# A fused attention and expert layer on one core: VectorE's dependent instructions laced with others, and two sums handed to TensorE and ScalarE

## The reference

```
h = layernorm(x) * (1 + ca) + sa
x = x + ga * attention(h)
h = layernorm(x) * (1 + cb) + sb
x = x + gb * experts(h)
```

```
pos  = clip(base + s_idx * freq_avg + phase_avg, 0, L - 1)
g    = g_lo + frac * (g_hi - g_lo)
out  = silu(einsum('blshd,blhs->blhd', g, w) @ out_w.T)
```

```
logits = h @ router_w.T + router_b
mask   = one_hot(top_k(softmax(logits), 2)).sum
out    = einsum('bse,ehd,bsd->bsh', mask, expert_w, h) + mask @ expert_b
```

## Time and profile before

| | us |
|---|---|
| three runs | 307.86, 310.82, 311.46 (median 310.82) |
| the profiled execution | 308.9 |
| its span on the core | 307.0 |
| busy TensorE / VectorE / ScalarE / GpSimd | 257.3 / 277.2 / 229.4 / 38.8 |
| mean granted TensorE clock | 0.898 of full |

### The profile page before, as it was taken

The page is one execution under the profiler, slowest core; times in us unless marked ns, Lnnn a source line. Parts: engine busy times, 40 slices in busy tenths (PEclk is TensorE's granted clock), DMA queues, the critical chain, the costliest instruction groups (busy, mean ns, idle before and its releaser), DMA issues.

```text
span 307.0 us, 5136 instructions
## 1 busy us (share of the span) xinstructions
PE 257.3 (84%) x1720; PEld 189.1 (62%) x1720; DVE 277.2 (90%) x570; ACT 229.4 (75%) x636; POOL 38.8 (13%) x64
## 2 busy tenths in 40 slices
PE   6970971999489998999699989999899959888995
PEld 3530830874388477857597568747784758475664
DVE  7799988999979899999999999999999999991772
ACT  3585788799868998898869988998679656845301
POOL 6204001200410011002020011002200400001100
PEclk9596697599958999899969997999699989999999
DMA  5630000020002200140005000500003000400001
GB/s 170 206 97 0 2 0 0 0 71 1 1 2 61 96 1 0 36 138 3 0 1 174 0 0 2 168 8 1 0 37 137 2 1 20 155 0 2 26 9 53
DMA packets 12160, 12.91 MB, mean 42 GB/s; under 512 B 1171, under 2 KB 11110, under 8 KB 11366
## 3 DMA queue, kind: packets, MB, share of 16 engines
q1 hardware_dynamic: 11684, 12.18, 12.8%
q10 hardware_dynamic: 450, 0.40, 0.5%
HBM read 10.43 MB, written 2.15 MB: 41 GB/s over the span
## 4 chain that ended last, share of the span: by engine, by line
DVE 50%; PE 22%; issue 14%; ACT 11%; POOL 2%; DVEq 0%; ACTq 0%; POOLq 0%
DVE AT L788 18%; DVE T L751 12%; PE pT L974 4%; DVE hm L849 4%; PE pR L974 3%; PE pY L1054 3%; ACT c L471 2%; DVE x L805 2%; PE pE L1054 2%; ACT xn L391 2%; DVE endw L776 2%; PE pR L951 2%; DVE x L854 1%; ACT hT L414 1%; DVE prodF L764 1%
## 5 line engine op out<-in xcount | busy, mean ns | idle before, releaser
L751 DVE COPY_PREDICATED T<-mask,T 128x672 f32<-128x672 int16 (+11 forms) x54 | 83.3, 1543 | 0.8
L788 DVE TENSOR_TENSOR AT<-T,c 128x2064 f32<-128x2064 f32 x32 | 72.3, 2301 | 0.0
L488 ACT ACTIVATE A<-pT 128x512 f32<-128x512 f32 x64 | 36.1, 599 | 27.6 <-PE pT L974 27.1
L974 PE MATMUL pT<-first,AT 128*128 128x128 f32 x256 | 43.9, 328 | 13.1 <-DVE AT L796 13.0
L1054 PE MATMUL pE<-hm,late 128*128 128x256 f32 x224 | 52.6, 386 | 0.0
L974 PEld LDWEIGHTS pT<-first,AT 128*128 128x128 f32 x256 | 37.3, 173 | 17.2 <-DVE AT L796 15.5
L1054 PEld LDWEIGHTS pE<-hm,late 128*128 128x128 f32 x224 | 41.2, 190 | 6.6
L974 PE MATMUL pR<-first,AT 128*128 128x128 f32 x256 | 40.4, 311 | 0.0
L315 POOL TENSOR_SCALAR ve<-sq 128x4 f32<-128x4 f32 (+1 forms) x18 | 8.8, 487 | 245.8 <-ACT xn L361 202.2
L488 ACT ACTIVATE A<-pR 128x512 f32<-128x512 f32 x64 | 35.8, 611 | 3.7 <-PE pR L974 3.6
L974 PEld LDWEIGHTS pR<-first,AT 128*128 128x128 f32 x256 | 36.0, 165 | 0.0
(11 more groups left out here) (139 smaller groups left out, 370.9 us busy)
## 6 DMA issues: line engine op xcount, KB each, us to landing
mkb<-mask_rows SPq DMA_DIRECT2D x6, 1024.0 KB, 5.4
x<-in_x SPq DMA_DIRECT2D x7, 256.0 KB, 5.6
out<-x SPq DMA_DIRECT2D x7, 256.0 KB, 5.7
late<-in_late SPq DMA_DIRECT2D x1, 584.0 KB, 3.9
mkb<-mask_rows SPq DMA_DIRECT2D x1, 512.0 KB, 3.8
x<-in_x SPq DMA_DIRECT2D x2, 128.0 KB, 3.5
wmod<-in_wmod ACTq DMA_DIRECT2D x1, 256.0 KB, 3.6
out<-x SPq DMA_DIRECT2D x2, 128.0 KB, 3.3
```

Of the source, the lines that this page charges most:

```text
L488: nc.scalar.activation(A[b][:, m, 2 * j:2 * j + 2, :].rearrange("p h l -> p (h l)"), four_banks(k)[:, :], ACT.Copy).then_inc(a_A, 1)
L751: nc.vector.copy_predicated(rows[:, :, :, j0:j1], spread(mask[:, k, 0:w, j0:j1], [P, w, H, j1 - j0], 2), rows[:, :, :, j0 + (1 << bit):j1 ...
L788: nc.vector.tensor_tensor(AT[:, bt, :, :].rearrange("p h (j r) -> p h j r", r=BLK), spread(T[n % 2][:, bt, 0:H, 0:NB], [P, H, NB, BLK], 3) ...
L974: ins = nc.tensor.transpose(four_banks(k)[:, c0:c0 + P], AT[:, 2 * b + i, 2 * j + a, m * P:(m + 1) * P], ident)
```

## The change

Four things.

- *Order on VectorE.* `ends_of`, `products`, `grid`, `route`, `sum_ends` and `spread_out` are cut into smaller stages, and these are called in another order, so that between an instruction and the one that reads its result there stands another. The products follow the first AT copy, the two products of hm come before the fourth and fifth network stage, the residual after the fifth.
- *Hits.* hit has 24 columns per index (erow repeated three times), and mk is gone. TensorE's back_mk takes the two hits of a tile through two matmuls with the identity that add up in the bank.
- *Last sum.* For units 0 to 5, back_out adds x (through the identity) to the transposed moeT in the bank, with two matmuls per tile instead of one transpose; ScalarE copies the bank to x (`total` on ScalarE). Units 6 to 8 keep VectorE's sum.
- *Order and filling.* On ScalarE, stats2 comes after front_hs and sums1. On TensorE, four matmuls of zeros (bf16, 512 columns) stand between back_x2T and back_logits.

```diff
-    c["erow"] = np.broadcast_to(np.arange(E, dtype=np.float32), (P, E)).copy()
+    c["erow"] = np.broadcast_to(np.tile(np.arange(E, dtype=np.float32), NP), (P, NP * E)).copy()
...
             def store(n):
-                sp.wait_ge(v_out, n + 1)
+                if n < LATE - 1:
+                    sp.wait_ge(a_out, n + 1)
+                else:
+                    sp.wait_ge(v_out, n - LATE + 2)
...
+            def total(n):
+                act.wait_ge(t_out, n + 1)
+                nc.scalar.activation(of_x(n), moe_bank(n)[:, 0:tiles(n) * C].rearrange("p (a c) -> p a c", c=C),
+                                     ACT.Copy).then_inc(a_out, 1)
...
-                run(i, -1, stats2)
                 if i >= 0:
                     run(i, 1, front_hs)
                 run(i, 2, sums1)
+                run(i, -1, stats2)
...
                 run(i, -1, back_mk)
+                run(i, -2, total)
                 run(i, 2, norm1)
...
-                dve.wait_ge(v_hit, n + 1)
+            def hits(n):
+                w = tiles(n)
+                dve.wait_ge(v_topi, LT * before(n + 1))
                 if n > 0:
                     dve.wait_ge(t_mk, n)
-                nc.vector.tensor_tensor(mk[:, 0:w, :].rearrange("p a (k e) -> p a k e", e=E),
-                                        spread(hit[:, 0:w, 0, :], [P, w, NP, E], 2),
-                                        spread(hit[:, 0:w, 1, :], [P, w, NP, E], 2), ALU.add).then_inc(v_mk, 1)
+                nc.vector.tensor_tensor(hit[:, 0:w, :, :], spread(spread(erow, [P, 2, NP * E], 1), [P, w, 2, NP * E], 1),
+                                        spread(topi[:, 0:w, 0:2], [P, w, 2, NP * E], 3), ALU.is_equal).then_inc(v_hit, 1)
...
-                run(i, 0, network, range(0, 2))
+                run(i, 0, network, range(0, 1))
...
-                run(i, 0, sum_ends)
-                run(i, 0, network, range(2, 4))
+                run(i, 0, sum_ends, 0)
+                run(i, 0, network, range(1, 2))
+                run(i, 0, sum_ends, 1)
+                run(i, 0, network, range(2, 3))
                 run(i, -2, masked, 0)
+                run(i, 0, network, range(3, 4))
+                second(i, -2, masked, 1)
                 run(i, 0, network, range(4, 5))
                 run(i, -1, residual)
-                second(i, -2, masked, 1)
                 run(i, 0, network, range(5, 6))
                 run(i, 1, line)
+                run(i, 0, spread_out, 0)
+                run(i, 1, past_ends)
+                run(i, 0, spread_out, 1)
                 run(i, 1, ends_of)
-                run(i, 1, products)
-                run(i, 0, spread_out, 0)
+                run(i, 0, set_ends, 0)
+                run(i, 1, product, 0, 0)
+                run(i, 1, product, 0, 1)
+                run(i, 1, product, 1, 0)
                 run(i, 1, grid)
-                run(i, -1, route)
-                second(i, 0, spread_out, 1)
-                run(i, -2, total)
+                run(i, -1, logits)
+                run(i, 1, offset)
+                run(i, -1, best)
+                run(i, 1, product, 1, 1)
+                run(i, -1, hits)
+                second(i, 0, spread_out, 2)
+                second(i, 0, spread_out, 3)
+                run(i, 1, cells_from)
+                second(i, 0, set_ends, 1)
...
             def back_mk(n):
-                pe.wait_ge(v_mk, n + 1)
+                pe.wait_ge(v_hit, n + 1)
                 for bt in range(tiles(n)):
-                    ins = nc.tensor.transpose(pL[0:NP * E, bt * P:(bt + 1) * P], mk[:, bt, :], ident)
+
+                    for k in range(2):
+                        ins = mm(pL[0:NP * E, bt * P:(bt + 1) * P], hit[:, bt, k, :], ident,
+                                 start=(k == 0), stop=(k == 1))
...
-                    ins = nc.tensor.transpose(moe_bank(n)[:, bt * P:(bt + 1) * P], moeT[:, bt * P:(bt + 1) * P], ident)
+                    dst = moe_bank(n)[:, bt * P:(bt + 1) * P]
+                    if n < LATE - 1:
+
+                        pe.wait_ge(v_x2, n + 1)
+                        mm(dst, ident, of_x(n)[:, bt, :], start=True, stop=False)
+                        ins = mm(dst, moeT[:, bt * P:(bt + 1) * P], ident, start=False, stop=True)
+                    else:
+                        ins = nc.tensor.transpose(dst, moeT[:, bt * P:(bt + 1) * P], ident)
...
                 run(i, -1, back_x2T)
+                if i > 0:
+                    warm_up(4, pT[0])
                 run(i, -1, back_logits)
```

More of the change, by code:

```diff
@@ L753, in network @@
                                               rows[:, :, :, j0 + (1 << bit):j1 + (1 << bit)]).then_inc(v_net, 1)
-            def products(n):
-                dve.wait_ge(v_kap, n + 1)
-                dve.wait_ge(a_row, LT * before(n + 1))
-                for q in range(LT):
-                    own = slice(q, tiles(n), LT)
-                    for far, (prod, count) in enumerate(((prodN, END), (prodF, FAR))):
-                        side = (q + far) % 2
-                        c0 = SHIFT[q] + (S - count if side else 0)
-                        ins = nc.vector.tensor_tensor(
-                            prod[:, own, :, :], T[n % 2][:, own, 0:H, c0:c0 + count],
-                            spread(kap[:, own, side, 0:count], [P, UNITS[n][1], H, count], 2), ALU.mult)
-                ins.then_inc(v_prod, 1)
@@ L769, in sum_ends, with product @@
-            def sum_ends(n):
+            def product(n, q, far):
+                if q == 0 and not far:
+                    dve.wait_ge(v_kap, n + 1)
+                    dve.wait_ge(a_row, LT * before(n + 1))
+                own = slice(q, tiles(n), LT)
+                prod, count = ((prodN, END), (prodF, FAR))[far]
+                side = (q + far) % 2
+                c0 = SHIFT[q] + (S - count if side else 0)
+                nc.vector.tensor_tensor(
+                    prod[:, own, :, :], T[n % 2][:, own, 0:H, c0:c0 + count],
+                    spread(kap[:, own, side, 0:count], [P, UNITS[n][1], H, count], 2), ALU.mult).then_inc(v_prod, 1)
@@ L770, in sum_ends @@
+            def sum_ends(n, far):
                 w = tiles(n)
-                dve.wait_ge(v_prod, n + 1)
+                dve.wait_ge(v_prod, 4 * (n + 1))
+                if n > 0:
+                    dve.wait_ge(v_end, before(n))
                 cells = endw[:, 0:w, :, :].rearrange("p (b t) e h -> p b (t e) h", t=LT)
-                for own, prod in ((slice(0, 4, 3), prodN), (slice(1, 3), prodF)):
-                    src = prod[:, 0:w, :, :].rearrange("p (b t) h s -> p b t h s", t=LT)
-                    ins = nc.vector.tensor_reduce(cells[:, :, own, :], src, AX.X, ALU.add)
@@ L777, in sum_ends, with spread_out @@
-                ins.then_inc(v_endw, 1)
-            def spread_out(n, b):
-                img = before(n) + b
-                if b == 0:
+                own, prod = ((slice(0, 4, 3), prodN), (slice(1, 3), prodF))[far]
+                src = prod[:, 0:w, :, :].rearrange("p (b t) h s -> p b t h s", t=LT)
+                nc.vector.tensor_reduce(cells[:, :, own, :], src, AX.X, ALU.add).then_inc(v_endw, 1)
+            def spread_out(n, bt):
+                b = bt // LT
+                if bt == 0:
@@ L809, in route, with logits @@
             def route(n):
+                logits(n)
+                best(n)
+                hits(n)
+            def logits(n):
                 w = tiles(n)
@@ L886, in _ @@
                     selectors()
-            network(LAST, range(0, 6))
+            network(LAST, range(0, 1))
+            sum_ends(LAST, 0)
+            network(LAST, range(1, 2))
+            sum_ends(LAST, 1)
+            network(LAST, range(2, 6))
             masked(LATE - 1, 0)
-            sum_ends(LAST)
             spread_out(LAST, 0)
+            spread_out(LAST, 1)
+            set_ends(LAST, 0)
             masked(LATE - 1, 1)
@@ L908, in _, with warm_up @@
             mm = nc.tensor.matmul
-            def warm_up(count):
+            def warm_up(count, bank=pE):
                 for _ in range(count):
-                    mm(pE[:, :], warm[:, 0:P], warm[:, :], start=True, stop=True)
+                    mm(bank[:, :], warm[:, 0:P], warm[:, :], start=True, stop=True)
             pe.wait_ge(v_zero, 1)
```

78 lines of the change are left out of this document (40 added, 38 removed).

## The result

| | median us | range of the runs |
|---|---|---|
| before | 310.85 | 307.86 to 311.46 |
| changed | 332.16 | 331.58 to 332.57 |

The ratio is 1.070, with a 95% interval of 1.064 to 1.076: 7% slower, where 304.0 with a range of 297 to 312 had been forecast. The profiled execution has a span of 330.7 us against 307.0.

The account below looks back on a forecast made before the run. VectorE set the pace at about 32.85 us per unit, TensorE under 2 us behind; afterwards TensorE would bind at 32.0. Terms -1.8 - 4.0 - 0.9 + 1.8 = -4.9 gave span 302.1, plus 1.9: 304.0 us, range 297 to 312.

Parts of the forecast that it names:

- the new period: TensorE's time per unit in the middle, the new bound: from 32.54 to 32.1, taken as 32.0 us.
- some 0.25 stay: TensorE's 0.70 us wait for xn2 in each unit: 0.5 goes, some 0.25 remains.
- the term of 3.7: From the start of stats2 on ScalarE to GpSimd's second layernorm factor: 3.7 us.
- the mask loop: Router, mask rows' DMA, masked product, residual, second layernorm, back to router: 31.3 us, under 32.0, so it costs nothing.
- VectorE saves 2.3 a unit: Closed gaps, removed mk step and moved last sum let VectorE do a unit in 30.55 instead of 32.85 us.
- A new matmul costs 0.22: Each added fp32 matmul on TensorE takes 0.22 us; hits and back_out each add 1.3 us per unit.
- The rival with dear matmuls: Added TensorE matmuls cost 0.44 us each and are the bound: period 35.5, total 322 us; chance 0.06.
- The clock: Less idling before mid_A should keep TensorE's clock full, saving 1.7 us per unit.
- The rival in which the dips stay: TensorE's clock still falls once per unit, 1.7 us on six periods: 314.2 us, 309 if in half; chance 0.14.
- The tail, +1.8: At the end, without laced cover, the last two units' hits stand on the path: +1.8 us.
- The start, -1.8: TensorE's first awaited copy comes 2.0 us earlier, the first low-clock warm-ups take some back: -1.8 us.

Follow-up runs that it names:

- experiment 5: Changed kernel, order untouched, with the second layernorm's factor for units 0 to 6 on VectorE instead of GpSimd, a reciprocal replacing the inverse root: 306.78 us, 0.991.
- experiment 4: Kernel before the change, with only the first image's AT products and copy moved ahead of the limits and end products: 310.07 us, 1.003.
- 1: Changed kernel with the whole old order of VectorE and ScalarE; hits, last sum and warm-ups stay moved: 307.81 us, 0.997 of before.
- 8: Changed kernel with stats2 first, the first image's AT behind the limits' products, masked products at their old places, other pairs still laced: 308.07 us, 0.996.
- 9: The kernel of 8 with the hits' sum also back on VectorE: 300.03 us, 0.972, the median of only two executions.
- 10: The kernel of 9 in the unlaced order of 1, leaving only the last sum in the bank and the warm-ups: 302.62 us, 0.979.
- experiment 2: Changed kernel with the first image's AT products and their copy put back behind the limits and end products: 320.86 us, 1.038.

## Why the prediction was wrong

**The step that failed** is in the paragraph on the new period: "GpSimd's factor comes at 179.25, 3.7 after the start of stats2 at 175.56 [...] some 0.25 stay". It carried the length of GpSimd's chain over from an order in which nothing held it, and used it again as the term of 3.7 in the mask loop, which so came to 31.3 and "costs nothing". Yet the step moved both ends together: stats2 later by 1.6, AT earlier by the products. That puts rs and nm beside the two AT products, where they took 5.1 instead of 1.6. On paper the loop had 0.7 of slack under the period of 32.0, and the hold is 3.5. In experiment 5 even this was not there: without any hold one turn of the loop took 32.1. The sum had left the loop no room for a longer term, and experiment 4 shows that as much hold costs some 1 us in all where there is room. Taking the factor off GpSimd (experiment 5) brought 306.8 us, a period of 32.1 and a wait of 1.2 for the mask rows: with GpSimd out of the loop, the period that was forecast is there, and the time lies in its range, 2.8 above the forecast.

**It could have been read from the kernel before.** GpSimd's timeline there has the same instructions at unequal lengths, and the long ones lie beside an AT product or a predicated copy:

```profile
27.89 2.95 POOL L317 TENSOR_TENSOR rs<-ve,mhalf 128x4 f32<-128x4 f32 x1
...
80.16 2.19 POOL L319 TENSOR_TENSOR nm<-mu,rs 128x4 f32<-128x4 f32 x1
...
241.76 1.84 POOL L315 TENSOR_SCALAR ve<-sq 128x4 f32<-128x4 f32 x1 [21.25 <-ACT xn L361]
```

So do the groups by shape shown above: a mean of 372 for an nm that takes 200 when free. The Trainium skill states the mechanism (SBUF — State Buffer, "SBUF: two separate sides"): VectorE and GpSimd share a pair of SBUF ports under an exclusive lock, which an operation of VectorE with two SBUF inputs holds against a GpSimd operation that reads SBUF, for the whole instruction. With that the traces agree in the rows above, where nm ends 0.05 after an AT product, whose two inputs T and c both lie in SBUF. They also hold a case that lasts longer than one instruction (last section). That the ports are what holds GpSimd is the page's statement; the runs show only when it is held.

**The other steps.**

- *VectorE saves 2.3 a unit.* Its busy time fell by 12.6 us, and the gaps closed (AT ends at 194.49, the small ones follow at 194.41, 194.55). But between experiments 1 and 8, ten executions each, the laced gaps are worth nothing that can be told, and between 9 and 10 the intervals overlap. The middle period is 31.8 to 32.2 in all four.
- *A new matmul costs 0.22.* Right: the eight of back_out follow each other in pairs of instructions mostly 0.22 to 0.25 apart, and the sixteen instructions of the hits need about 1.8. But in the last units the hits cost more than their matmuls (next but one). The rival with dear matmuls (322) came nearer to the time by accident; its mechanism is refuted by experiments 1 and 5.
- *The clock.* That the dips would go was right only where TensorE is not kept waiting: 1.00 in the middle of experiment 5, 0.92 in the changed kernel, hardly more than the 0.91 before. The rival in which the dips stay did happen in the changed kernel, as a consequence of TensorE's wait for the norm, since the clock was full once that was gone.
- *The tail, +1.8,* was too small: in experiments 1 and 10, which differ in the hits alone, they cost 3.8 us of span behind 245 us. *The start, -1.8,* no run takes apart.
- *The mask loop.* It was named, and rightly summed in its DMA and its masked products, but given as slack, with no rival that asked what would make it longer. The rival on the slower side was looked for in TensorE's work alone.

## What to carry to other kernels

Before an instruction of one engine is moved, look at what then runs beside it on an engine that shares something with it: a 4-element instruction of GpSimd can take as long as a large two-input product of VectorE, or two. A duration from the trace holds for its neighbours in that trace; where one kind of instruction has several lengths there, find what lies beside the long ones before one of them enters a sum. And where two loops are within a microsecond of each other, closing 0.1 us gaps in one bought nothing here, while each term of the other must be good to less than its slack. A lengthened instruction is to be judged by that slack: 13 us more of it than before cost one kernel 1 us and were part of a loss of 21 us in another.

## What the runs showed of the hardware

- A held GpSimd instruction can be passed over by several of VectorE's. In experiment 2 an nm that started at 197.36 came through only at 202.03, 0.09 after the short product near (201.61 + 0.33) that followed two AT products without a gap. In the changed kernel, where the two AT products have the product fe between them, rs came through 0.86 after the first product's end, so about its own free length of 1.01 later. The gap is not what decides: in experiment 4 two AT products also ran without one, from 178.35, and nm came through at 180.72, as the first, 2.30 long, ended. What lets it in at one boundary and not at another is left open.
- The hold seems to come from predicated copies too (in the kernel before ve took 1.84 and ended at 243.60, with the copy's 243.58).
- Neither side shows the hold as a wait: the profile books it as busy time of GpSimd. It is seen in the mean of a group, and in two ends that coincide. VectorE's AT product takes 2.30 us whether it holds GpSimd or not.
